# Attention with decay masks and a mixture of experts on one core: where the scores stand in TensorE's order within a tile's step

## The reference, cut to what matters

```python
x = x + tanh(g_xattn[0]) * xattn(layernorm(x), ctx, ctx, Wi, bi, Wf, bf, ln_scale)
x = x + tanh(g_ffn[0])  * ffn(layernorm(x), ...)      # router, top 2 of 16 experts, shared expert

# xattn, per sequence and head (s, t tokens; d = 32)
log_D = log_fg + transpose(ig)            # lower triangle of sums of log forget gates, -inf above
D = exp(log_D - max(log_D, -1))           # "decay"
qk = einsum('bhsd,bhtd->bhst', qh, kh) / sqrt(dh)     # "scores"
C = qk * D
Cn = C / (max(abs(C.sum(-1)), exp(-max_log_D)) + EPS)
h = einsum('bhst,bhtd->bhsd', Cn, vh)     # "values' products"
hn = (h - mu) * rsqrt(var + EPS) * ln_scale
```

## Time and profile before

| | |
|---|---|
| runs (3), median | 775.14 us (774.03 to 776.44) |
| the profiled execution | 775.68 us, of it 773.9 us in the span of the trace |
| PE busy | 691.8 us (89% of the span) |
| PE weight load busy | 603.0 us (78%) |
| DVE busy | 506.0 us (65%) |
| ACT busy | 411.1 us (53%) |
| POOL busy | 392.3 us (51%) |
| attention, from tile 0's decays to tile 31's values' products | 86.8 us to 294.2 us |

### The profile page before, as it was taken

The page is one execution under the profiler, slowest core; times in us unless marked ns, Lnnn a source line. Parts: engine busy times, 40 slices in busy tenths (PEclk is TensorE's granted clock), DMA queues, the critical chain, the costliest instruction groups (busy, mean ns, idle before and its releaser), DMA issues.

```text
span 773.9 us, 19573 instructions
## 1 busy us (share of the span) xinstructions
PE 691.8 (89%) x7407; PEld 603.0 (78%) x7408; DVE 506.0 (65%) x1007; ACT 411.1 (53%) x851; POOL 392.3 (51%) x592
## 2 busy tenths in 40 slices
PE   0877498899899887999999999999999999999994
PEld 0644377777777766778899998999999999999993
DVE  4758278987777698866259795534566676766650
ACT  0667467686766674434362332223466656666651
POOL 2410377888888774521112542223355766667554
PEclk9999699999999998999999999999999999999998
DMA  7885464446555710687633222423678888979864
GB/s 248 276 277 173 120 191 142 155 143 183 143 161 168 229 41 28 203 303 277 236 104 110 59 86 75 118 88 105 200 223 237 226 257 229 238 225 240 256 130 54
DMA packets 90212, 134.55 MB, mean 174 GB/s; under 512 B 16704, under 2 KB 43840, under 8 KB 90144
## 3 DMA queue, kind: packets, MB, share of 16 engines
q1 hardware_dynamic: 73472, 106.04, 42.9%
q0 software_dynamic: 7168, 17.04, 11.1%
q10 hardware_dynamic: 9504, 10.55, 4.4%
HBM read 92.06 MB, written 33.95 MB: 163 GB/s over the span
## 4 chain that ended last, share of the span: by engine, by line
PE 68%; DVE 8%; ACT 4%; DMA 4%; issue 3%; POOL 1%; SPq 0%; ACTq 0%; POOLq 0%; DVEq 0%
PE psH L1302 30%; PE psY L1322 15%; PE psQ L719 4%; PE ring L736 4%; PE psO L764 4%; PE ring L704 2%; PE ring L730 2%; ACT dec L806 2%; PE psT L1282 2%; DMA out<-ystage,sidx 1%; DMA xT<-over13l 1%; DVE dec L886 1%; PE psR L1349 1%; DVE xl L1551 1%; ACT sq L830 1%
## 5 line engine op out<-in xcount | busy, mean ns | idle before, releaser
L1302 PE MATMUL psH<-xh,w13h 128*128 128x256 f32 (+1 forms) x768 | 220.8, 288 | 2.8 <-issue 2.8
L1302 PE MATMUL psH<-xh,w13l 128*128 128x256 f32 (+1 forms) x768 | 215.5, 281 | 0.0
L1302 PE MATMUL psH<-xl,w13h 128*128 128x256 f32 (+1 forms) x768 | 215.1, 280 | 0.0
L1794 POOL TENSOR_TENSOR hl<-sg,hh 128x256 fp32r<-128x256 f32 (+1 forms) x96 | 79.5, 837 | 177.9 <-ACT hh L1425 177.4
L1302 PEld LDWEIGHTS psH<-xh,w13h 128*128 128x128 f32 (+1 forms) x768 | 138.0, 180 | 11.3 <-issue 10.4
L1302 PEld LDWEIGHTS psH<-xl,w13h 128*128 128x128 f32 (+1 forms) x768 | 138.3, 180 | 0.8
L1302 PEld LDWEIGHTS psH<-xh,w13l 128*128 128x128 f32 (+1 forms) x768 | 138.0, 180 | 0.0
L886 DVE SCALAR_TENSOR_TENSOR dec<-psQ,dec 128x512 f32<-128x512 f32 x128 | 79.5, 683 | 44.2 <-PE psQ L719 44.1
L1420 ACT ACTIVATE sg<-psH 128x256 f32<-128x256 f32 (+1 forms) x96 | 36.4, 379 | 126.0 <-PE psH L1302 125.3
L1557 DVE TENSOR_TENSOR sg<-sg,psH 128x256 f32<-128x256 f32 (+1 forms) x96 | 40.0, 416 | 95.4 <-ACT sg L1420 95.4
L806 ACT ACTIVATE dec<-ring 128x512 f32<-128x512 f32 x128 | 71.2, 596 | 17.6 <-PE ring L707 17.1
(11 more groups left out here) (228 smaller groups left out, 1410.5 us busy)
## 6 DMA issues: line engine op xcount, KB each, us to landing
raw<-w13T SPq DMA_DIRECT2D x64, 352.0 KB, 4.4
gcT<-ctxT ACTq DMA_DIRECT2D x8, 1024.0 KB, 6.1
kT<-ctxT SPq DMA_DIRECT2D x16, 512.0 KB, 4.2
ctxs<-ctx SPq DMA_DIRECT2D x16, 512.0 KB, 3.8
xn<-xnorm SPq DMA_DIRECT2D x16, 512.0 KB, 3.3
out<-xres SPq DMA_DIRECT2D x16, 512.0 KB, 4.9
raw<-w2T SPq DMA_DIRECT2D x16, 512.0 KB
qst<-qT_all SPq DMA_DIRECT2D x14, 512.0 KB, 5.0
```

Of the source, the lines that this page charges most:

```text
L1302: last = nc.tensor.matmul(psH[m][0:n, v, :], w[wp][:, c, col:col + n], x[xp][:, c, :], start=(c == 0 and k == 0), stop=(c == DC - 1 and k ...
L1794: nc.gpsimd.tensor_tensor(hs[u.p][1][0:n, m, :], sg[0:n, m, :], hs[u.p][0][0:n, m, :].bitcast(F32), ALU.subtract).then_inc(hl_ready, 1)
```

## The change

Only the order of TensorE's queue within a step changes. Before, the scores stand behind decay 2 (and behind the state's gathering in an odd step). After, the scores stand directly behind the values' products of the preceding tile, then comes the state's gathering, then decays 2 and 3 together. No instruction is added or taken away, and no other engine's list changes.

```diff
@@ -770,13 +770,12 @@
                 if r >= 1:
                     ring_free(use(OUT))
                     values(i, r - 1, bank(r, OUT))
+                queries(i, r)
+                if r % 2 == 1:
+                    gather_state(i, r)
                 for k in range(2):
                     ring_free(use(last2(r) + k))
                     decay(i, r, 2 + k, bank(r, last2(r) + k))
-                    if k == 0:
-                        if r % 2 == 1:
-                            gather_state(i, r)
-                        queries(i, r)
                 if r >= 1:
                     back(i, r - 1, use(OUT))
                 if not is_last:
```

## The result

The changed kernel takes 781.41 us (median of 4 runs, 779.41 to 783.06) where the kernel before takes 775.37 (774.03 to 776.44): ratio 1.0088, 95% interval 1.0057 to 1.0118. Slower, as forecast; 782 was predicted. Two later measurements, each against the kernel before in the same session, gave 1.0123 (1.0102 to 1.0144) and 1.0115 (1.0084 to 1.0145), so the change costs 6 to 9 us.

What follows compares the result with a forecast made beforehand. Odd steps were taken as bound by a TensorE-ScalarE loop (products, back, square, exponential 0), with ScalarE's state copy nearly tied; 6.0 - 0.3 + 0.3 + 1.5 - 0.5 = +7.0 us gave 782 us, own range 779.5 to 789.4, 8-in-10 range 778.5 to 790.

Steps and rivals of the forecast that it cites:

- Odd steps: Ten odd steps: gathering 0.66 us later delays ScalarE's state copy and square; 0.60 us each (0.52 to 0.66), 6.0 in all.
- the clock rival: Longer TensorE waits before the state's products in odd steps lower its clock: 787.4 us, 798 if all do; chance 0.18.
- Even steps: 14 even steps: L707 no longer lies beneath the scores, so back and square come 0.11 us later; 1.5 us in all.
- Step 11: ScalarE was late by its gates; the gathering's new place passes it by 0.3 us: +0.3 us.
- Step 0: Scores no longer stand behind decay 2's wait for GpSimd's table, and first values' products wait for the weighings: -0.5 us.
- The term that the trace did not show: TensorE idling when scores directly follow values' products: taken as 0, with 0.20 x 31 = 6.2 us as upper end.
- Steps 7 to 9: Gathering waits for VectorE's `take` in 7 and 9: step 7 -0.3 us, step 9 nothing; in step 8 VectorE decides.
- Steps 27, 29 and 31: Nothing: a DMA wait covers the delay in 27; products wait for VectorE's weighings behind mixture work in 29 and 31.
- a sign of being wrong: A granted TensorE clock below 1 between 95 and 250 us was listed among the findings that would show the prediction wrong.
- The forecast sum: Over the whole kernel: 6.0 - 0.3 + 0.3 + 1.5 - 0.5 = +7.0 us, giving 782 us.
- The loop goes through the scores: Values' products wait for the last weighing, not exponential 0, so earlier scores gain 12.9 us: 762.2 us; chance 0.05.
- The gathering's delay is covered: ScalarE has half a microsecond to spare ahead of the square, leaving +0.7 us, 775.8 us; chance 0.07.

Runs made afterwards that it cites:

- odd only: The changed kernel with the new order in odd steps alone, even steps in the order of before: 778.73 us, ratio 1.0080.
- gathering last: The kernel before, but in odd steps the state's gathering stands behind the scores (values' products, decay 2, scores, gathering, decay 3): 784.32 us, ratio 1.0121.
- gathering first with even steps as before: The changed kernel, with odd steps in the order gathering, scores, decays 2 and 3, and even steps as in the kernel before: 779.39 us, ratio 1.0079.
- even only: The changed kernel with the new order in even steps alone, odd steps in the order of before: 772.69 us, ratio 0.9994.
- gathering first: The changed kernel, but in odd steps the state's gathering stands directly behind the values' products and the scores behind it: 773.41 us, ratio 0.9992.
- decay 0 early with early scores: The changed kernel with odd steps' gathering ahead of the scores, next tile's decay 0 ahead of the back, its exponential ahead of root and square: 775.34 us, 1.0019.
- decay 0 early with the old scores: The kernel before with next tile's decay 0 ahead of the back and its exponential ahead of root and square: 772.72 us, 0.9961; again 772.83, 0.9987.

## Why the prediction was right

**Odd steps: right, and its size nearly.** The ten that count grew by 5.4 us together (second profiles, for step 1 the first: 0.47 to 0.50 outside the loop, 0.38 in step 13, 0.55 to 0.65 in it) where 6.0 was forecast. Outside the loop that is just beneath the stated bounds of 0.52 and 0.66: the cover was 0.16 us, and 0.14 had been taken as the most. The gathering began 2.11 us after the products (2.1 forecast), the square 111.30 - 106.18 = 5.12 us after (5.1 to 5.2 forecast).

**A wait that I missed.** I wrote that the back stays where it is. It doesn't: `back` waits for the state's copy (`state_taken`, L759), since both use `psO`. That wait had been hidden 0.3 us deep. It cost the time nothing more, because ScalarE's own queue reached the square no sooner than the moved back would have let it, 0.1 us apart at most: in the chain the root (L836, L837), and not the back, stands ahead of the square. No run took either of the two alone away. But it changed where TensorE idles, and so the clock rival's premise. Outside the loop, in place of one wait of about 1.0 us there are two of 0.44 and 0.42, and the granted clock stayed at the upper level, 2.4 GHz, in the steps from 100 to 290 us in all three profiles. In the loop the first is 0.44 to 0.54, and the second is hardly longer than the 0.59 in the earlier trace rows:

```profile
202.37 1.13 PE L730 MATMUL ring<-qsc,state 128*128 128x128 f32 x8 [0.65 <-ACT dec L805]
```

**Even steps: right.** 14 steps grew by 1.5 us together, as forecast, 0.11 us for L707 in most. **Step 11: right**, +0.29. **Step 0: right**: from the end of the wait for GpSimd's table to the first values' products it is 4.88 us where it was 5.38 (first profiles). **The term that the trace did not show**, scores directly behind values' products, is nothing, as taken: the scores begin 1.01 us after the products (107.19 - 106.18), as the decay did in their place (107.01 - 106.00).

**Steps 7 to 9: the direction right, the size too small.** Step 7 gained 0.84 us (forecast 0.3), step 8 0.22 and step 9 0.17 (forecast 0). I had taken the gates' instructions on VectorE as given. Two of them were stretched by GpSimd, against the earlier trace rows; before:

```profile
130.16 1.16 DVE L539 TENSOR_SCALAR gates<-gates 128x256 f32<-128x256 f32 x1
...
137.54 1.15 DVE L543 SCALAR_TENSOR_TENSOR gates<-gates 128x256 f32<-128x256 f32 x1
```

```profile
130.12 1.05 POOL L1012 TENSOR_TENSOR numc<-numc,sm 128x512 f32<-128x512 f32 x1
```

and after:

```profile
131.09 0.31 DVE L539 TENSOR_SCALAR gates<-gates 128x256 f32<-128x256 f32 x1
...
137.63 0.42 DVE L543 SCALAR_TENSOR_TENSOR gates<-gates 128x256 f32<-128x256 f32 x1
```

```profile
131.64 1.13 POOL L1011 TENSOR_TENSOR numc<-numc,sm 128x512 f32<-128x512 f32 x1
```

Before, L539 lay on a GpSimd instruction that ended at 131.17, and itself ended at 131.32. After, it was over before GpSimd's began. The other kernels take the two apart. Step 7 takes 6.91 to 7.53 us in every profile in which L539 is stretched (both of the kernel before, odd only, gathering last, gathering first with even steps as before) and 5.80 to 6.25 in all others. Step 8 takes 6.65 or 6.66 in the three in which L543 is (both of the kernel before, even only) and 6.28 to 6.44 in all others.

The Trainium skill, page SBUF — State Buffer, section "SBUF: two separate sides", says that VectorE and GpSimd share one pair of ports as an exclusive lock held for a whole instruction, so that the loser waits till the other is done. It says this of VectorE's instructions in a two-port mode or with two inputs in SBUF. The traces agree, with 0.31 us alone and 1.16 beside, ending 0.15 us after GpSimd's; L543 has two inputs in SBUF, and no run shows in which mode L539 ran.

**Steps 27, 29 and 31: nothing forecast, -0.5, -0.5 and +0.7 measured.** Step 27 is the DMA above. In steps 29 and 31 VectorE and GpSimd work for the mixture meanwhile. Each kernel's lengths repeat from profile to profile, but why step 29 gains and step 31 loses no run took apart.

**What the sum left out: TensorE's clock, its cause open.** Steps 2 to 31 grew by 5.2 us (194.3 against 189.1), step 1 by 0.5 in the first profile, step 0 shrank by 0.5, and the medians differ by 6 to 9. In the profiles the rest lies in step 1 and behind the attention, where the granted clock is lower. Of six profiles in which the scores open step 0, five show TensorE's clock at the lower level for longer (in the changed kernel's second profile until about 96 us instead of 92), and then step 1 takes 7.5 to 7.8 us: the second and third of the changed kernel, gathering first, even only, and decay 0 early with early scores. Of seven in which decay 2 opens it, three have a step 1 of 6.6 to 8.2 us (gathering last, and both of decay 0 early with the old scores). These are too few to tell. And in the 50 us behind the attention the granted clock differs from run to run. Windows of the kernel before (second) and of the changed one (second); stretch, its us, busy us of PE, PEld, DVE, ACT, POOL, granted clock, share of the DMA engines, GB/s:

```profile
288.00:298.00 10.00, 7.05 (x81) 5.71 (x82) 7.97 (x17) 4.53 (x11) 3.64 (x12) 1.00 0.14 54
298.00:313.00 15.00, 11.94 (x103) 10.21 (x104) 14.86 (x30) 8.29 (x18) 9.71 (x10) 1.00 0.23 89
313.00:338.00 25.00, 22.22 (x187) 18.34 (x185) 17.28 (x45) 10.73 (x25) 8.29 (x8) 1.00 0.81 281
```

```profile
295.00:305.00 10.00, 7.12 (x57) 6.16 (x58) 5.64 (x12) 3.64 (x8) 3.17 (x9) 0.67 0.14 54
305.00:320.00 15.00, 13.91 (x112) 11.86 (x111) 14.82 (x31) 7.89 (x16) 10.38 (x13) 0.90 0.09 36
320.00:345.00 25.00, 23.22 (x180) 19.78 (x177) 18.00 (x47) 11.43 (x26) 7.43 (x8) 0.86 0.75 270
```

From the last products' start to the end it is 482.3 us in the first and 485.3 in the second, but 483.4 and 483.6 in the first profiles of before and after. In the third profile of the changed kernel it is 485.3 again. Unlucky profiles are not the reason, for every run of those two measurements says the same. The mean granted clock was 0.964 to 0.974 in all ten runs of the changed kernel's two later measurements. In the kernel before, measured in the same sessions, it was 0.973 to 0.983 in 23 runs and 0.968 to 0.981 in 17. Odd only, with the same odd steps but decay 2 first in step 0, had 0.971 to 0.983 and lost 5.5 us where the changed kernel lost 9.2. So the changed kernel does get the lower clock more often. What in it brings that about, in step 0 or behind the attention, no run took apart. Behind the attention it is worth up to 3 us of the difference, in step 1 up to 1.9, and neither was in the forecast's sum.

**Luck in the number.** The forecast sum was +7.0 us. With the terms as they came out (odd steps 5.4, steps 7 to 9 -1.2, step 11 +0.3, even steps 1.5, step 0 -0.5, steps 27 to 31 -0.3) it is about +5.2, and the three medians stand 1 to 4 us above that. The median of 781.41 lies within 1 us of 782 because a gain that was sized too small and a cost that was left out went opposite ways.

**The rivals.** "The loop goes through the scores" fell: the weighings began earlier and waited 0.80 us for exponential 2. "The gathering's delay is covered" fell but for 0.16 us. The clock's fall did not come in the odd steps, where I put it, but in step 1 and behind the attention. In the second and third profile it was still low at 96 us, just inside the stretch from 95 to 250 us in which the prediction had called a low clock a sign of being wrong. The price of that rival also left out a fourth long wait that stands in the earlier trace rows: after 2.19 us the products of tile 31 took 2.05 us instead of 1.13, so two of the four waits read were followed by the lower clock, not one of three.

## What to carry to other kernels

When an instruction is moved ahead of another, price what now stands behind it, not only what it frees: the scores gained nothing, and the small gathering that they passed fed ScalarE's queue, in which everything up to the end of the step stands behind the state's copy. Read the cover of a delay from a step in which that cover was used up (here 2.46 us against 2.60), and list every wait of the engines that follow, those hidden by 0.3 us too. Step lengths from the timeline repeat within 0.1 us from profile to profile in most steps, where whole runs tell 2 us. But they hold only for the steps that they measure: here they miss what the clock did in front of them and behind.

## What the runs showed of the hardware

A VectorE instruction of 0.31 us on [128, 256] took 1.16 us when it met a GpSimd product of [128, 512], in two profiles of the kernel before and again in the odd-only, gathering-last and gathering-first-even-as-before kernels, and 0.30 to 0.33 in the eight profiles in which it missed it.

How long TensorE idled does not tell whether its clock falls. In the middle of the attention the granted clock went to the lower level after waits of 1.15 us (step 27, kernel before, first profile), 1.67 and 1.79 us (steps 27 and 9, gathering first with even steps as before) and 2.38 us (step 27, decay 0 early with old scores, second profile). It stayed at the upper one after 1.27 and 1.50 us, and after 1.72, 1.88 and 2.15 us (step 7 of gathering first with even steps as before, and step 27 of decay 0 early with early and with old scores). The same wait of one kernel went both ways: 2.19 us ahead of tile 31's products in the first profile of the kernel before, with products of 2.05 us, and 2.18 in the second, with products of 1.13.
